# Conditioned attention and adapter kernel: causal mask by VectorE, values as eight array tiles, and a new order of values, router and stores

## The reference

```
att   = softmax(mlp(cond));  agg_w, agg_b = att-weighted 32x32 matrices and biases
y     = einsum('boi,bih->boh', agg_w, x) + agg_b           # mixes the 32 positions of a sequence
q,k,v = rope(y @ Wq), rope(y @ Wk), y @ Wv                 # 32 query heads, 8 key heads, 16 wide
x1    = x + softmax(causal(q k^T / 4)) v @ Wo
z     = grouped_conv1d(x1, 9 taps, 4 groups) + context     # over the 32 positions as channels
out   = x1 + z @ base_W^T + base_b + lora                  # lora weighted by a router's top 8 of 15
```

## Time and profile before

| | |
|---|---|
| median of 3 runs | 653.37 us (650.11, 653.37, 654.2) |
| the profiled execution | 651.24 us, span 649.3 us, mean granted clock 0.988 |
| PE (TensorE) | 616.8 us busy, 95% of the span, 4363 matmul records |
| DVE (VectorE) | 474.8 us, 73%, 1169 instructions |
| ACT (ScalarE) | 200.3 us, 31%, 475 instructions |
| POOL (GpSimd) | 224.6 us, 35%, 181 instructions |
| hardware DMA queue | 70.89 MB in 86016 packets, 45.6% of 16 engines |
| load of the late biases (mixb) | 1792.0 KB, 8.9 us to landing |
| load of base_W | 1024 KB, in the first 60 us |

### The profile page before, as it was taken

How to read it: one execution, slowest core, us unless ns; L and a number is a source line. 1 busy time by engine, 2 the same in 40 slices (tenths; PEclk the granted TensorE clock), 3 DMA queues, 4 the chain that set the end, 5 groups by cost and what they waited for, 6 DMA issues and landing times.

```text
span 649.3 us, 12985 instructions
## 1 busy us (share of the span) xinstructions
PE 616.8 (95%) x4363; PEld 508.9 (78%) x4363; DVE 474.8 (73%) x1169; ACT 200.3 (31%) x475; POOL 224.6 (35%) x181
## 2 busy tenths in 40 slices
PE   5984999999999999999999999999999999999876
PEld 4663788888888888888888888888888888888654
DVE  3565577788777777787877777787777777887742
ACT  4342232333323323233223323233233323333210
POOL 7353133333333332333333332333333333333310
PEclk9998899999999999999999999999999999999998
DMA  7658334445554344444553334454543434454430
GB/s 173 121 145 238 74 84 94 106 120 118 122 122 105 89 97 96 107 121 118 122 119 100 93 90 95 118 120 120 122 111 90 97 95 101 120 118 106 107 83 32
DMA packets 87509, 71.57 MB, mean 110 GB/s; under 512 B 48342, under 2 KB 70518, under 8 KB 84169
## 3 DMA queue, kind: packets, MB, share of 16 engines
q1 hardware_dynamic: 86016, 70.89, 45.6%
q10 hardware_dynamic: 1336, 0.24, 0.2%
q0 software_dynamic: 144, 0.28, 0.2%
HBM read 51.86 MB, written 19.53 MB: 110 GB/s over the span
## 4 chain that ended last, share of the span: by engine, by line
PE 88%; DMA 6%; DVE 3%; SPq 1%; ACT 1%; issue 1%; DVEq 0%
PE ps L398 34%; PE ps L571 9%; PE ps L565 8%; PE ps L624 6%; PE ps L591 5%; PE ps L583 5%; PE ps L498 4%; PE ps L612 4%; PE ps L535 3%; DMA x_dram<-x1p 3%; DMA scratch<-x_dram 2%; PE ps L599 2%; PE ps L555 2%; PE ps L579 1%; PE ps L538 1%
## 5 line engine op out<-in xcount | busy, mean ns | idle before, releaser
L889 POOL TENSOR_TENSOR qk<-network,t 128x640 f32<-128x640 f32 x31 | 48.3, 1559 | 171.2 <-DVE t L1066 171.2
L398 PE MATMUL ps<-wqkv_hi,y_hi 128*128 128x512 f32 (+1 forms) x256 | 87.3, 341 | 2.3 <-DVE raw L1085 1.5
L398 PE MATMUL ps<-wqkv_hi,y_lo 128*128 128x512 f32 (+1 forms) x256 | 87.1, 340 | 0.0
L398 PE MATMUL ps<-wqkv_lo,y_hi 128*128 128x512 f32 (+1 forms) x256 | 86.9, 340 | 0.0
L901 POOL TENSOR_TENSOR raw<-x1p,basebB 128x512 f32<-128x512 f32 x32 | 49.2, 1538 | 100.9 <-DVE x1p L1140 100.9
L1074 DVE TENSOR_TENSOR qk_t<-ps,cst 128x512 f32<-128x512 f32 x32 | 22.1, 692 | 67.1 <-PE ps L553 67.1
L714 ACT ACTIVATE qk_t<-ps 128x512 f32<-128x512 f32 x32 | 19.1, 598 | 142.5 <-PE ps L555 142.5
L714 ACT ACTIVATE raw<-ps 128x256 f32<-128x256 f32 (+1 forms) x96 | 40.2, 453 | 66.2 <-PE ps L612 64.5
L776 ACT ACTIVATE raw<-raw 128x512 f32<-128x512 f32 x64 | 40.6, 634 | 54.3 <-DVE raw L1085 54.3
L398 PEld LDWEIGHTS ps<-wqkv_hi,y_hi 128*128 128x128 f32 x256 | 48.6, 190 | 10.0 <-DVE raw L1085 2.7
L873 POOL TENSOR_TENSOR raw<-raw,rz 128x512 f32<-128x512 f32 x32 | 33.7, 1052 | 65.1 <-DVE rz L1095 65.1
(11 more groups left out here) (180 smaller groups left out, 1482.7 us busy)
## 6 DMA issues: line engine op xcount, KB each, us to landing
scratch<-x_dram SPq DMA_DIRECT2D x96, 259.8 KB, 4.3
x_dram<-x1p SPq DMA_DIRECT2D x32, 260.0 KB, 4.5
xm<-x SPq DMA_DIRECT2D x32, 256.0 KB, 3.8
xr<-x SPq DMA_DIRECT2D x32, 256.0 KB, 4.0
out<-raw SPq DMA_DIRECT2D x32, 256.0 KB, 2.1
v_dram<-vS SPq DMA_DIRECT2D x32, 64.0 KB
vB<-v_dram SPq DMA_DIRECT2D x128, 16.0 KB, 2.2
mixb<-mixb_dram SPq DMA_DIRECT2D x1, 1792.0 KB, 8.9
```

Source lines behind the costliest of these rows:

```text
L398: last = mm(dst, a, b, start=(n == 0), stop=(n == 3 * len(left) - 1))
L889: nc.gpsimd.tensor_tensor(qk[:, :], t1, t2[:, :], ALU.add).then_inc(qk_sb, 1)
```

## The change

- The mask matmuls and their two bf16 constants are no longer used; VectorE adds the mask to the scores while it moves them to SBUF, and takes maximum and difference there, in place. TensorE may reuse a scores bank once that addition is done.
- The router's `route` (logits and maximum) comes ahead of `normalize`.
- The values are sixteen matmuls of 64 rows and 32 columns each instead of eight of 128 and 64. For odd sequences the two pairs of key heads change places, in the keys' mask and in `vS`. The output lies in banks 4 and 7. They come after conv, wait for `hwT_lo` and for both copies of P, and in the hardware loop one matmul of two columns in conv's shape goes ahead of them.
- Transposed P lies in banks 2 and 4 and is copied in two pieces; `oT_hi` and `oT_lo` are made in two pieces, `vS` in six.
- Project takes the products of the high part of its input first and waits for the low part only before the last four.
- `x1_dram` has x1's four rows of a partition side by side. SyncE loads V behind xc, stores V ahead of x1, and loads the late weights and biases after x1's store, the biases in two parts in iterations 1 and 2.

```diff
-        vB = sb("vB", [P, NB, 2, HK * HD])
+        vB = sb("vB", [P, NB, 2, 2 * HD])
...
-        x1_dram = nc.dram_tensor("x1_dram", [CG * PH, NB * PH, P + 2], F32, kind="Internal").ap()
+        x1_dram = nc.dram_tensor("x1_dram", [NB * PH, CG * PH, P + 2], F32, kind="Internal").ap()
...
+        def heads(w, a):
+            return w[:, :, :, :].rearrange("p g (b a) q -> p a g b q", a=2)[:, a, :, :, :]
+        def heads_ps(a):
+            return ps[:, 4 + 3 * a, 0:2 * P].rearrange("p (b g q) -> p g b q", b=NB // 2, g=NQ)
...
             def steps(t):                                   # SyncE
...
                     for s in range(SHIFTS):
-                        sp.dma_start(xcF[S * s:S * (s + 1), 0:x1_row],
-                                     x1_dram.rearrange("r q n -> r (q n)")[:, s:s + x1_row]).then_inc(xc_in, 16)
-                if live(t + 1):
-                    load_values(t + 1)
-                if peeled(t, 0):
-                    late_mixing()
+                        sp.dma_start(xc[S * s:S * (s + 1), :, :],
+                                     x1_dram[:, :, s:s + P].rearrange("q r n -> r q n")).then_inc(xc_in, 16)
+                if live(t) and not peeled(t, 0):
+                    load_values(t)
...
+                if live(t + 1):
+                    store_values(t + 1)
                 if live(t):
                     sp.wait_ge(x1_sb, t + 1)
-                    sp.dma_start(x1_dram.rearrange("r q n -> q r n"), x1p[:, :, :]).then_inc(x1_out, 16)
+                    sp.dma_start(x1_dram.rearrange("q (i j) n -> (q i) j n", j=PH), x1p[:, :, :]).then_inc(x1_out, 16)
                 if live(t) and live(t + 1):
                     sp.dma_start(xr[:, :], group(x_g, t + 1)).then_inc(xr_in, 16)
+                if peeled(t, 0):
+                    sp.wait_ge(mixw_out, 16)
+                    load_mixw(sp, 4, G, mixw_in)
+                if peeled(t, 1):
+                    late_bias(4, 12)
+                if peeled(t, 2):
+                    late_bias(12, G)
...
             def queries(u):                                 # TensorE
                 if live(u - 1):
-                    pe.wait_ge(sx_sb, 2 * (u - 1) + 1)
+                    pe.wait_ge(sm0_sb, 2 * (u - 1) + 1)
...
             def project(u):
                 pe.wait_ge(oT_hi_sb, u + 1)
-                pe.wait_ge(oT_lo_sb, u + 1)
-                o = [...]
-                product(ps[:, 3, :], o, [(wo_hi[:, g, :], wo_lo[:, g, :]) for g in range(NQ)]).then_inc(wo_ps, 1)
+                wait(pe, x1_sb, u)
+                for n, (a, b) in enumerate(((oT_hi, wo_hi), (oT_hi, wo_lo), (oT_lo, wo_hi))):
+                    if n == 2:
+                        pe.wait_ge(oT_lo_sb, u + 1)
+                    for g in range(NQ):
+                        last = mm(ps[:, 3, :], a[:, g, :, :].rearrange("p b q -> p (b q)"), b[:, g, :],
+                                  start=(n == 0 and g == 0), stop=(n == 2 and g == NQ - 1))
+                last.then_inc(wo_ps, 1)
...
             def scores(t):
-                for h in range(2):
-                    rows = slice(h * P // 2, h * P // 2 + S)
-                    mm(ps[:, h, :], query16[rows, :], causal16[rows, :], start=True, stop=False)
...
             def transpose_p(t):
-                wait(pe, x1_sb, t)
...
             def values(t):
                 pe.wait_ge(vB_in, 16 * HK * (t + 1))
+                if live(t - 2):
+                    pe.wait_ge(hwT_lo_sb, t - 1)
+                if peeled(t, 0):
+                    pe.wait_ge(prep_sb, 1)
+                if peeled(t, 1):
+                    pe.wait_ge(base_lo_sb, 2)
+                pe.wait_ge(pT_sb, 2 * t + 2)
+                if not isinstance(t, int):
+                    mm(ps[0:S, 4, 0:2], convW[:, 0, :, :].rearrange("p j o -> p (j o)"), xc[:, 0, 0:2], start=True, stop=True)
                 for b in range(NB):
-                    if b != 2:
-                        pe.wait_ge(pT_sb, 3 * t + (1, 2, 2, 3)[b])
                     for h in range(2):
-                        last = mm(ps[P // 2 * h:P // 2 * (h + 1), 4, b * P:(b + 1) * P], vB[:, b, h, :], prT[:, 2 * b + h, :],
-                                  start=True, stop=True)
+                        for r in range(2):
+                            rows = slice(2 * S * r, 2 * S * (r + 1))
+                            to = S * (2 * h + (r + b) % 2)
+                            last = mm(ps[to:to + S, 4 + 3 * (b % 2), b // 2 * P:(b // 2 + 1) * P],
+                                      vB[rows, b, h, :], prT[rows, 2 * b + h, :], start=True, stop=True)
                 last.then_inc(o_ps, 1)
...
             def steps(t):                                   # TensorE: order behind transpose_p
                 if peeled(t, G - 1):
-                    values(t)
+                    conv(t - 1)
...
                 if live(t - 2):
                     transpose_hw(t - 2)
-                if live(t) and not peeled(t, G - 1):
-                    values(t)
...
-                if live(t - 1):
+                if live(t - 1) and not peeled(t, G - 1):
                     conv(t - 1)
                 if peeled(t, G):
-                    keep_warm(3)
+                    keep_warm(2)
+                if live(t):
+                    values(t)
                 if peeled(t, 1):
+                    pe.wait_ge(oT_lo_sb, 2)
                     prepare_base((2, 3))
...
+            def keep_values():                              # ScalarE
+                for b in range(NB):
+                    rows = slice(S * b, S * (b + 1))
+                    if b % 2 == 0:
+                        copy(vS[rows, :], ps[rows, 1, P:2 * P])
+                        continue
+                    pairs, pairs_ps = (w.rearrange("p (h r d) -> p r h d", h=2, r=2) for w in (vS[rows, :], ps[rows, 1, P:2 * P]))
+                    for r in range(2):
+                        last = copy(pairs[:, r, :, :], pairs_ps[:, 1 - r, :, :])
+                last.then_inc(vS_sb, 1)
...
             def softmax(t):                                 # VectorE
                 for h in range(2):
...
-                    v.tensor_reduce(m, s3, AX.X, ALU.max).then_inc(mx_sb, 1)
+                    sx3 = sx[:, D * h:D * h + D].rearrange("p (h m) -> p h m", m=S)
+                    v.tensor_tensor(sx3, s3, cst[:, C_CAUSAL:C_CAUSAL + S].unsqueeze(1).broadcast_to([P, 16, S]),
+                                    ALU.add).then_inc(sm0_sb, 1)
+                    dve.wait_ge(sm0_sb, 2 * t + 1 + h)
+                    v.tensor_reduce(m, sx3, AX.X, ALU.max).then_inc(mx_sb, 1)
                     dve.wait_ge(mx_sb, 2 * t + 1 + h)
-                    v.tensor_tensor(sx[:, D * h:D * h + D].rearrange("p (h m) -> p h m", m=S), s3,
-                                    m.unsqueeze(2).broadcast_to([P, 16, S]), ALU.subtract).then_inc(sx_sb, 1)
+                    v.tensor_tensor(sx3, sx3, m.unsqueeze(2).broadcast_to([P, 16, S]), ALU.subtract).then_inc(sx_sb, 1)
...
                 if live(t):
                     softmax(t)
+                if live(t - 2):
+                    route(t - 2)
+                if live(t):
                     normalize(t)
...
                 if live(t - 2):
-                    route(t - 2)
                     route2(t - 2)
```

More of the change, by code:

```diff
@@ L45 @@
 C_KV = C_CAUSAL + S
-C_SEQ = C_KV + HK
+C_SEQ = C_KV + NB * HK
 C_COS = C_SEQ + NB
@@ L543, in project @@
                 pe.wait_ge(oT_hi_sb, u + 1)
-                pe.wait_ge(oT_lo_sb, u + 1)
-                o = [tuple(w[:, g, :, :].rearrange("p b q -> p (b q)") for w in (oT_hi, oT_lo)) for g in range(NQ)]
-                product(ps[:, 3, :], o, [(wo_hi[:, g, :], wo_lo[:, g, :]) for g in range(NQ)]).then_inc(wo_ps, 1)
+                wait(pe, x1_sb, u)
[6 more added lines that the diff above has]
+                last.then_inc(wo_ps, 1)
             def transpose_qk(t):
@@ L583, in scores @@
                         last = mm(ps[:, h, b * P:(b + 1) * P], qT[rows, b, :, :].rearrange("p g q -> p (g q)"),
-                                  kT[rows, b, :, :].rearrange("p k m -> p (k m)"), start=False, stop=(b == NB - 1))
+                                  kT[rows, b, :, :].rearrange("p k m -> p (k m)"), start=True, stop=True)
                         if b == NB - 1:
@@ L606, in transpose_p @@
                     pe.wait_ge(ys_sb, t + 2)
-                wait(pe, x1_sb, t)
                 for b in range(NB):
                     for h in range(2):
-                        n = 2 * b + h
-                        bank, at = ((2, n), (3, n - 2), (3, n - 2), (5, n - 6))[b]
-                        last = nc.tensor.transpose(ps[:, bank, at * P:(at + 1) * P],
+                        at = 2 * (b % 2) + h
+                        last = nc.tensor.transpose(ps[:, 2 + 2 * (b // 2), at * P:(at + 1) * P],
                                                    pr[:, (NB * h + b) * P:(NB * h + b + 1) * P], ident)
-                    if b != 1:
+                    if b % 2:
```

(26 more changed lines are left out.)

29 lines of the change are left out of this document (14 added, 15 removed).

## The result

The changed kernel takes 669.77 us (median of 4 runs, 669.29 to 670.82), the kernel before 652.76 in 4 runs beside it: ratio 1.026 [1.023, 1.029]. It is slower by 17 us, and above the range of the prediction. The profiled execution took 669.46 us, its span is 667.6, 18.3 more than before, at a mean granted clock of 0.978.

What follows compares the result with a forecast made beforehand. TensorE, holding 88% of the chain of waits, was taken as the bound, with VectorE's results only 0.60 us early. 28 x 0 - 1 (filling) - 1 (draining) = -2 us from 651.24 gave 649.2, forecast as 650, range 638 to 662.

Steps and rivals of the forecast that it cites:

- filling: First iterations: earlier x1 store against later values, longer softmax chain and second bias load; net -1 us, from -5 to +2.
- contention on the first subtraction: VectorE's softmax: subtraction reading SBUF twice beside GpSimd's y_lo; 0.25 us for both subtractions, ends 0 and 0.4.
- TensorE waits for `hw`: Middle iteration, at L631: the slack of 0.60 us becomes a wait of 0.3 to 0.6 us.
- TensorE resumes behind it: Between the end of `hwT_lo` and TensorE's next work, ahead of the values: about 0.12 us.
- small matmul and values: TensorE behind conv: 0.10 us for the added matmul and 0.65 us for the tiled values, sum 0.75 us.
- x1 store to landing: Store of x1 in 2080-byte rows: lands in 2.5 us, 2 us less than the 4.5 us before.
- draining: Last iterations: two stores of x1 lie on the chain with their loads; -1 us, from -2 to +1.
- 28 x 0: Steady loop: 28 middle periods stay at 18.35 us, TensorE's lost work offset by waiting; from 17.95 to 18.8.
- As cheap as they can be: Rival, chance 0.36: tiles and SBUF reads without contention, values 0.50 us, 0.3 to 0.4 us less per period, 641 us.
- Values gain no overlap: Rival, chance 0.17: array tiles bring no overlap, values take 1.02 us, period 18.72, time 660 us.
- Short rows: Rival, chance 0.06: 512-byte load pieces over 65 ns each make conv wait 0.3 us per iteration, 658 us.
- a VectorE that is never late: Bound for the middle loop: period 17.5 us and time 627, which the slack of 0.60 us spoke against.

Runs made afterwards that it cites:

- The earlier loading: Changed kernel with the late biases loaded one iteration earlier, the 0.5 MB part in iteration 0 and the 1.3 MB part in iteration 1: 665.39 us, ratio 1.019.
- the kernel with `hwT_lo` earlier: Changed kernel with `hwT_lo` computed between the two sine products of RoPE instead of behind them: 659.48 us, ratio 1.013.
- the old layout: Changed kernel with x1's DRAM layout as before, 520-byte pieces stored and long rows loaded, queue order kept: 676.79 us, ratio 1.041.
- late router: Changed kernel with the router's logits and maximum behind P's normalisation again: 714.19 us, ratio 1.093.
- mask-alone kernel: Kernel before with only the mask's move: VectorE adds the mask, TensorE no longer does: 679.94 us, ratio 1.046.

## Why the prediction was wrong

The mechanism of the period was right, two of its sizes and one rounding were not, and the filling's wait was looked for in the wrong place. The measured period, 18.77 us, still lies inside the predicted 17.95 to 18.8; what took the time out of the range was the filling on top of it. Point by point, with the changed kernel's middle iteration laid on that of the earlier trace rows (322.39 on 311.87):

| step | predicted | measured |
|---|---|---|
| softmax starts | 315.09 | 315.03 |
| contention on the first subtraction | 0.25 (0 to 0.4) | 1.19 - 0.69 = 0.50 |
| `hw` ends | 324.24 | 324.39 |
| TensorE waits for `hw` | 0.3 to 0.6 | 0.54 |
| `hwT_lo` ends | 325.71 | 325.85 |
| TensorE resumes behind it | 0.12 | 336.62 - 336.37 = 0.25 |
| small matmul and values | 0.75 | 0.14 + 0.60 = 0.74 |
| LoRA and project | 0.92 + 2.85 | 0.91 + 2.88 |
| period | 18.35 | 18.77 |
| x1 store to landing | 2.5 | 2.0 |
| filling | -1 (-5 to +2) | +6 (in this execution) |
| draining | -1 | +1 |

**The step that failed first is the sum of the period, "28 x 0".** Its terms give 325.71 + 0.12 + 0.75 + 0.92 + 2.85 = 330.35, which is 0.13 us above the old period; it was rounded to 330.3 and then to nothing. 28 times 0.13 are 3.6 us. The range had the same slip: its ends, 329.9 and 330.8, are 18.03 and 18.93 us after 311.87. The contention adds 0.14 us at `hwT_lo` (0.25 more than predicted on the subtraction, less 0.06 for the softmax's start and some hundredths along the chain), the resuming 0.13, the stages behind it 0.01: with the rounding's 0.13, that is 0.41 of the 0.42 us. The contention was scaled from P's normalisation, where 0.12 us stood beside 0.26 of overlap. That proportion does not hold: y_lo had 327.62 - 326.99 = 0.63 us to go when the subtraction started, and 0.50 of it was lost. The Trainium skill, SBUF — State Buffer, section "SBUF: two separate sides", has a VectorE instruction with two SBUF inputs and a GpSimd instruction that reads SBUF take turns: the one that starts second waits for the whole of the other. By that the subtraction would end at 327.62 + 0.69 = 328.31; it ended at 328.18. The trace is nearer to the lock than to my proportion, and y_lo itself was not longer (1.29 us against 1.30). With the lock in the sum my upper end for contention would have been 0.6 and not 0.4.

**The step that failed worst for its size is the filling.** I gave the second bias load "up to 2 us" in front of conv's input. It was not conv that waited. VectorE waits for both parts ahead of y of group 4, which reads only the first. The second was issued at 93.44 and landed 6.6 us later: 7.90 us of idle time. TensorE in turn stood still for 6.39 us ahead of its queries, and the granted clock was 0.50 from 100 to 106 us, so that its next matmuls came 0.43 us apart in place of 0.23; this is how 6.39 us of waiting become an interval that is 8.2 us longer. The other half of this term held: the x1 store was issued at 48.77 and conv started at 60.23 (47.3 and 59.5 forecast), and iteration 2 was 2.0 us ahead, so +8.2 - 2.0 = +6. I had followed the moved DMA along SP's queue, but not to its reader. The earlier loading gives back 4.4 us of it by the medians, and no placing tried gives back all.

**The draining** was to gain 1 us and lost about 1. The longer chain on VectorE is paid there too: in the last group TensorE waits 3.23 us for the normalised P, where it waited 1.64 us before. Behind that wait the granted clock is 0.50 from 632 to 640 us. In the kernel with `hwT_lo` earlier the same wait is 3.21 us, the clock stays at 1.00, and the last three intervals take 41.35 us, 4.4 less; why the clock stays up there is open. The layout's gain, shown by the old layout's 48.85 - 45.74 = 3.1 us, hid part of the loss.

**The rivals.** "As cheap as they can be" fell with the 0.50. "Values gain no overlap" named the nearest time, 660, for a false reason: the values took 0.60 us, where it needed 0.9. The Trainium skill, TensorEngine Tiling (Array Packing), section Performance Considerations, gave at least 0.8 us by its 60 cycles a matmul; the trace does not agree, 32 records went in 0.60 us, 19 ns each. "Short rows" fell too: conv waits for no DMA in the middle, and the layout is a gain. The bound named for a VectorE that is never late, a period of 17.5 us, was right in size: with the mask on TensorE 17.83 was measured, and 0.32 of it are the mask matmuls.

**Left open.** The small matmul was not taken out by itself. The 0.25 us from the end of `hwT_lo` to TensorE's next record were measured, but what they consist of was not; behind `hw` the same step takes 0.06 us (334.91 to 334.97). Why 16 of the late router's iterations lost the clock and the others did not stays open as well.

## What to carry to other kernels

Before work is moved to a less busy engine, read the slack of that engine's results at the consumer: here 0.60 us, against 1.44 us of additions for 0.32 us of TensorE. Of every operand that changes from PSUM to SBUF, look at what GpSimd runs at that moment, and of every DMA that is moved, at its last reader and not only at its neighbours in the queue. A sum that comes out at 0.1 us per iteration is not zero when the loop runs 32 times.

## What the hardware showed beyond this

- The price of two SBUF inputs beside GpSimd is 0.50 us on a 0.69 us instruction (1.19), and none with one of the inputs in PSUM (0.69) beside the same y_lo, which itself takes 1.29 us in both.
- The granted clock stayed at 1.00 (2.4 GHz) in the middle of the mask-alone kernel, with one wait of 1.18 us in each iteration. It fell to 0.50 (1.2 GHz) in 16 of 26 iterations of the late-router kernel, for instance where TensorE waited 1.22 us and, one conv later, 0.35 us, and such an iteration was 1.5 us longer. The other ten had waits of the same length and kept the clock, and the two kernels differ in more than the second wait; what decides is not shown. At the end of the changed kernel the clock fell behind a wait of 3.23 us, and in the kernel with `hwT_lo` earlier it did not behind one of 3.21.
- Storing x1 in pieces of 2080 bytes took 2.0 us, in pieces of 520 bytes 4.4. The Trainium skill, DMA: Bandwidth & Descriptors, section Specifications, names 512 bytes as the least transfer for line rate; the 520-byte pieces were above it and still took twice as long. Loading in pieces of 512 bytes instead of long rows cost 5.0 against 4.3 us.
